# Rounds of a mixture-of-experts router: the inverse root of the variance moved from GpSimd to ScalarE and VectorE, the gate columns moved from VectorE to ScalarE

## The reference

```python
# layer 4 (x: 32 x 256 tokens of 128)
mu = mean(x); var = mean((x - mu)**2)
xn = (x - mu) * rsqrt(var + 1e-5) * gamma + beta
logits = xn @ Wr + br                       # 8 experts
top_vals, top_idx = top_k(logits, 2)
w = softmax(top_vals)                       # two gates per token
y = sum over the two experts e of w_e * (gelu(xn @ W1[e] + b1[e]) @ W2[e] + b2[e])
x = x + y
```

## Time and profile before

| what | value |
|---|---|
| time, median of 3 runs | 862.75 us (860.98 to 864.96) |
| the profiled execution: its own time | 861.31 us |
| its span, first to last instruction | 859.5 us |
| busy: TensorE, VectorE, ScalarE, GpSimd | 688.8, 618.1, 431.6, 310.8 us |
| mean granted TensorE clock | 0.697 |

### The profile page before, as it was taken

One profiled execution on the slowest core, in us unless ns is written; L12 is line 12 of the kernel. 1 busy time (PEld: TensorE's weight loads), 2 busy tenths in 40 slices (PEclk: granted clock), 3 DMA queues, 4 the chain that ended last, 5 costly groups with the idle time before them and its releaser, 6 DMA issues.

```text
span 859.5 us, 23527 instructions
## 1 busy us (share of the span) xinstructions
PE 688.8 (80%) x7545; PEld 494.4 (58%) x7545; DVE 618.1 (72%) x3004; ACT 431.6 (50%) x1572; POOL 310.8 (36%) x486
## 2 busy tenths in 40 slices
PE   0895898888887878788888888987783699998993
PEld 0774665545444445454545454576672388887883
DVE  5334777777777777777777777476775299998994
ACT  1113555444444444545454545244442288887882
POOL 4700112222232322232212112228776355555553
PEclk9997655555555555555555555689987699999997
DMA  4993111111111011111110111445522333443430
GB/s 128 163 233 120 32 32 45 32 44 32 42 31 43 31 40 34 40 33 41 32 43 31 43 31 31 135 122 171 159 93 81 112 93 105 109 114 96 112 87 1
DMA packets 75404, 64.39 MB, mean 75 GB/s; under 512 B 8344, under 2 KB 72189, under 8 KB 75309
## 3 DMA queue, kind: packets, MB, share of 16 engines
q1 hardware_dynamic: 67715, 50.31, 22.4%
q0 software_dynamic: 5984, 12.74, 4.2%
q10 hardware_dynamic: 1636, 0.48, 0.3%
HBM read 37.94 MB, written 27.32 MB: 76 GB/s over the span
## 4 chain that ended last, share of the span: by engine, by line
PE 42%; DVE 28%; ACT 17%; issue 9%; POOL 1%; another core or an unknown queue 1%; DMA 0%; DVEq 0%; SPq 0%; POOLq 0%; ACTq 0%
PE pb L813 10%; DVE pb L1462 8%; ACT tanh_c L1132 5%; DVE h L1464 5%; ACT GC L1128 4%; PE pb L1014 4%; ACT S L1130 3%; PE pb L850 3%; PE pb L1016 2%; PE pb L1015 2%; PE pb L1030 2%; PE pb L1031 2%; PE pb L1029 2%; ACT adjT L1147 2%; PE pb L727 2%
## 5 line engine op out<-in xcount | busy, mean ns | idle before, releaser
L813 PEld LDWEIGHTS pb<-h,vp 128*128 128x128 bf16 x3840 | 142.5, 106 | 190.7 <-DVE h L1464 187.7
L813 PE MATMUL pb<-h,vp 128*128 128x32 f16 x3840 | 171.5, 190 | 54.7 <-DVE h L1464 41.8
L691 POOL DMA_INDIRECT out<-outb,out_i x91 | 92.5, 1016 | 83.4 <-DVE outb L1647 62.1
L782 PE MATMUL pb<-xbuf,us 128*128 128x256 f32 x198 | 117.5, 699 | 0.0
L1128 ACT ACTIVATE GC<-pb 128x32 f32<-128x32 f32 x256 | 51.0, 199 | 130.1 <-PE pb L813 130.1
L1462 DVE TENSOR_TENSOR_SCAN pb<-S,GC 128x64 f32<-128x64 f32 x256 | 77.3, 302 | 32.5 <-ACT S L1130 18.5
L1132 ACT ACTIVATE tanh_c<-pb 128x32 f32<-128x32 f32 x256 | 50.5, 197 | 96.0 <-DVE pb L1462 96.0
L1464 DVE SCALAR_TENSOR_TENSOR h<-S,tanh_c 128x32 f16<-128x32 f32 x256 | 49.2, 192 | 67.4 <-ACT tanh_c L1132 67.4
L1635 DVE SCALAR_TENSOR_TENSOR glo<-Gl,pw,ghi 128x512 f16<-128x512 f32 x91 | 68.4, 752 | 19.0 <-ACT ghi L1244 11.6
L1014 PE MATMUL pb<-xT,w 128*128 128x128 f16 x364 | 66.4, 221 | 10.5 <-issue 5.5
L679 POOL DMA_INDIRECT xs_d<-stg,slot x64 | 62.9, 983 | 31.3 <-issue 17.7
(11 more groups left out here) (331 smaller groups left out, 1629.0 us busy)
## 6 DMA issues: line engine op xcount, KB each, us to landing
Xp<-xs_d SPq DMA_DIRECT2D x91, 130.0 KB
adjn<-in_adj SPq DMA_DIRECT2D x32, 256.0 KB, 2.7
x_d<-x2s SPq DMA_DIRECT2D x33, 128.0 KB, 1.8
y_d<-ys SPq DMA_DIRECT2D x33, 128.0 KB, 1.8
X<-in_x SPq DMA_DIRECT2D x4, 912.0 KB, 18.4
xs_d<-zrow SPq DMA_DIRECT2D x1, 3640.0 KB, 13.8
yr<-y_d SPq DMA_DIRECT2D x8, 256.0 KB
x2r<-x_d SPq DMA_DIRECT2D x8, 256.0 KB
```

Of the source, the lines that this page charges most:

```text
L691: pool.indirect_dma_start(out_rows, bass.IndirectOffsetOnAxis(out_i[t % 4][:, 0:1], 0), outb[t % 4][:], None, bounds_check=B * T - 1, oob_ ...
L782: mm(o, us[:, q, :], xbuf[:], start=False, stop=False, skip_group_check=True)
L813: return mm(o, vp[p][:, q, :], h[:], start=False, stop=True, skip_group_check=True)
```

## The change

In rounds 2 to 7 the inverse root comes by another way. VectorE stores a quarter of the variance term (rounds 0 and 1 keep the whole one and GpSimd's power). ScalarE's `take_root` takes the square root of it; the two one-element activations around it put ScalarE's table loads where they stand. VectorE's `scale(F)` then makes one correction step: with v the stored quarter and r the root, `v/r + r` is the corrected whole root, and its reciprocal is `rs_m`. `nb_m` follows at once, so it is made at the end of rows(F) and no longer inside route. GpSimd keeps only the powers of rounds 0 and 1. The gate columns `0.5 +- 0.5*tanh` are written by ScalarE behind the tanh, and GpSimd's send waits for them (`gates_set`).

```diff
@@ GpSimd @@
                 if half == 0:
                     pool.wait_ge(slot_ready, F + 1)
+                    pool.wait_ge(gates_set, F + 1)
...
             for F in range(NF):
                 send(F, 0)
-                if F + 2 < NF:
-                    norm_scale(F + 2)
                 send(F, 1)
@@ ScalarE @@
             def router_tanh(F):
                 act.wait_ge(dif_ready, F + 1)
                 av(th[F % 2][:], hdif[F % 2][:], ACT.Tanh).then_inc(th_ready, 1)
+                act.wait_ge(th_ready, F + 1)
+                av(stg[F % NBUF][:, :, 2 * P], th[F % 2][:], ACT.Identity, scale=half_k, bias=half_k)
+                av(stg[F % NBUF][:, :, 2 * P + 1], th[F % 2][:], ACT.Identity, scale=minus_k[:, 0:1], bias=half_k).then_inc(gates_set, 1)
+
+            def take_root(F):
+
+                av(spare[:, 0, F:F + 1], ident[:, 0:1], ACT.Sqrt)
+                act.wait_ge(m_aggr, F + 1)
+                av(root[F % 2][:], ve_m[F % 2][:], ACT.Sqrt).then_inc(root_ready, 1)
+                av(spare[:, 1, F:F + 1], ident[:, 0:1], ACT.Tanh)
...
                     normed_evacuate(2 * F + 2)
                     normed_evacuate(2 * F + 3)
+                    if F + 2 < NF:
+                        take_root(F + 2)
@@ VectorE @@
-                v.tensor_scalar(ve_m[F % 2][:], mv_m[F % 2][:, :, 1], LN_EPS, SC ** -2, ALU.add, ALU.mult).then_inc(m_aggr, 1)
+                v.tensor_scalar(ve_m[F % 2][:], mv_m[F % 2][:, :, 1], LN_EPS, SC ** -2 * (0.25 if F >= 2 else 1.0), ALU.add, ALU.mult).then_inc(m_aggr, 1)
...
+            def scale(F):
+
+                k = F % 2
+                dve.wait_ge(root_ready, F - 1)
+                link(v.reciprocal(quot[:], root[k][:]))
+                link(v.tensor_tensor(quot[:], ve_m[k][:], quot[:], ALU.mult))
+                link(v.tensor_tensor(quot[:], quot[:], root[k][:], ALU.add))
+                link(v.reciprocal(rs_m[k][:], quot[:]))
                 v.scalar_tensor_tensor(out=nb_m[k][:], in0=mv_m[k][:, :, 0], scalar=-1.0, in1=rs_m[k][:], op0=ALU.mult, op1=ALU.mult).then_inc(nb_ready, 1)
...
-                if F + 1 < NF:
-                    shift(F + 1)
+                if F == 0:
+                    shift(1)
...
-                dve.wait_ge(th_ready, F + 1)
-                v.tensor_scalar(stg[n][:, :, 2 * P], th[k][:], half_k, half_k, ALU.mult, ALU.add)
-                v.tensor_scalar(stg[n][:, :, 2 * P + 1], th[k][:], minus_k[:, 0:1], half_k, ALU.mult, ALU.add)
...
                 if F + 2 < NF:
                     rows(F + 2)
+                    scale(F + 2)
```

More of the change, by code:

```diff
@@ L253, in build @@
         mv_m, ve_m, rs_m, nb_m = (ring(n, 2, [P, NT] + s) for n, s in (("mv_m", [2]), ("ve_m", []), ("rs_m", []), ("nb_m", [])))
-        half8 = sb("half8", [P, NT])
+        half8, quot, root = sb("half8", [P, NT]), sb("quot", [P, NT]), ring("root", 2, [P, NT])
+        spare = sb("spare", [P, 2, NF])
         lg, top, top_i = sb("lg", [P, NT, E]), sb("top", [P, NT, E]), sb("top_i", [P, NT, E], U32)
@@ L305, in build @@
         adj_loaded = [sem(f"adj_loaded{i}") for i in range(2)]
-        (ht_ps, hts_ready, c_ps, x3_ready, m_aggr, rs_ready, nb_ready, xh_ready, xhT_ps, xnT_ready,
-         logits_ps, brg_ps, brg_ready, dif_ready, th_ready, oneh_ready, rank_ps, rank_read, count_ps, slot_ready, wrg_ready,
+        (ht_ps, hts_ready, c_ps, x3_ready, m_aggr, rs_ready, root_ready, nb_ready, xh_ready, xhT_ps, xnT_ready,
+         logits_ps, brg_ps, brg_ready, dif_ready, th_ready, gates_set, oneh_ready, rank_ps, rank_read, count_ps, slot_ready, wrg_ready,
          beta_ready, fold_ps, folded_w, biased, prep_ready, squares_ready, folded_ready, mx_ps, mx_ready, powers_ready, tri_ready,
@@ L311, in build @@
          xt_ps, xT_ready, xl_ready, l1_ps, gelu_ready, ghi_ready, glo_ready, l2_ps, out_ready) = (sem(n) for n in (
-            "ht_ps", "hts_ready", "c_ps", "x3_ready", "m_aggr", "rs_ready", "nb_ready", "xh_ready", "xhT_ps", "xnT_ready",
-            "logits_ps", "brg_ps", "brg_ready", "dif_ready", "th_ready", "oneh_ready", "rank_ps", "rank_read",
+            "ht_ps", "hts_ready", "c_ps", "x3_ready", "m_aggr", "rs_ready", "root_ready", "nb_ready", "xh_ready", "xhT_ps", "xnT_ready",
+            "logits_ps", "brg_ps", "brg_ready", "dif_ready", "th_ready", "gates_set", "oneh_ready", "rank_ps", "rank_read",
             "count_ps", "slot_ready", "wrg_ready", "beta_ready", "fold_ps", "folded_w", "biased", "prep_ready", "squares_ready", "folded_ready",
@@ L1533, in shift @@
                 dve.wait_ge(rs_ready, F + 1)
+                v.scalar_tensor_tensor(out=nb_m[k][:], in0=mv_m[k][:, :, 0], scalar=-1.0, in1=rs_m[k][:], op0=ALU.mult, op1=ALU.mult).then_inc(nb_ready, 1)
+            def scale(F):
[5 more added lines that the diff above has]
+                link(v.reciprocal(rs_m[k][:], quot[:]))
                 v.scalar_tensor_tensor(out=nb_m[k][:], in0=mv_m[k][:, :, 0], scalar=-1.0, in1=rs_m[k][:], op0=ALU.mult, op1=ALU.mult).then_inc(nb_ready, 1)
```

## The result

The changed kernel takes 880.05 us (median of 4 runs, 879.73 to 883.87) against 863.36 us of the kernel before, measured beside it: ratio 1.021, 95% interval 1.018 to 1.024. That is slower by 17 us, outside the predicted range of 857 to 871. Its profiled execution took 880.01 us, with a span of 878.2.

A forecast was written before the change was run, and what follows sets the result against it. The rounds were taken as bound by a VectorE-ScalarE-TensorE loop setting the last slots, not by busy GpSimd. lg delays of +4.05, less 0.6 and 0.25, gave +3.2 us: 864.5 or 866.0 by baseline, forecast 865.5, range 857 to 871.

The forecast's parts named there:

- The terms of the chain: Per round, from last evacuation to lg: 0.2 for gates, 1.66 to the root, 0.96 on VectorE, together +2.82 us.
- Root after the evacuation: On ScalarE in each round with a root: it is ready 1.66 us after the evacuation ends.
- The table load: On ScalarE behind the last evacuation: 1.28 us, next activation 0.02 behind it; the load back is hidden.
- The semaphore: Last term of the root's path on ScalarE: 0.05 us.
- The figure of the Trainium skill: ScalarE's table switch at about 2.66 us: root some 1.4 us later each round, sum near +9; not adopted.
- Gate writes: Two ScalarE activations ahead of normalise's second half: 0.28 us each, 0.6 with the wait; evacuations 0.2 later, between 0 and 0.8.
- the sum of +3.2 us: Net delay over the rounds: lg delays of +4.05, less 0.6 for nb_m and 0.25 for VectorE's gate writes.
- the removed part: Six powers leave GpSimd's queue, 9.5 us, worth nothing while VectorE's last slots come as late as now.
- inside the stall: Rounds 1 and 3: VectorE's existing stalls ahead of lg cover the root's longer path, so each adds 0.
- signs of being wrong: Wrong if "remote" waits vanish or move, the first reciprocal doesn't wait, or the rounds' granted clock is well under 0.9.
- The rival on the stalls: VectorE's stalls in the rounds belong to GpSimd's power and go with it: -1.7 to -5.3 us, 857.4; chance 0.25.
- The clock rival: TensorE waits longer in the rounds and its clock falls: 1.7 us per such round, about +6, 871; chance 0.20.

The follow-up runs named there:

- e1: The kernel before with ScalarE writing the gate columns, powers left on GpSimd: 864.44 us, ratio 1.003.
- e4: The kernel before with ScalarE's root and table loads added behind the evacuations, result unused, powers left on GpSimd: 861.74 us, ratio 1.000.
- e9: The changed kernel as it is, measured again in a group without late signals: 844.5 us, ratio 0.999 to the kernel before.
- e15: The changed kernel with an idle GpSimd power between the halves of each round's transfers, rounds 0 to 5; late signals: 866.52 us, ratio 1.006.
- e17: The changed kernel with scale moved from ahead of route (the suspected place) into route, transfers in runs of eight; late signals: 887.19 us, ratio 1.024.
- warm: The changed kernel with three idle matmuls ahead of each round's places: ratio 0.995 to 0.996 without late signals, 1.018 with them.
- e18: The changed kernel with three idle matmuls ahead of each round's places, in a group with late signals: 876.6 us, ratio 1.018.
- e11: The changed kernel with an idle GpSimd power between the halves of each round's transfers, without late signals: 846.72 us, ratio 1.001.
- in_route: The changed kernel with scale moved inside route, where shift was, transfers in runs of eight: ratio 0.995 to 0.996 without late signals, 1.024 with them.
- e7: The changed kernel with scale inside route and an idle GpSimd power between each round's transfer halves, without late signals: 845.45 us, ratio 1.001.
- e6: The changed kernel with scale inside route, transfers in runs of eight, without late signals: 840.2 us, ratio 0.995.

## Why the prediction was wrong, point by point

**The terms of the chain were right.** Root after the evacuation: 595.61 - 593.99 = 1.62 us, predicted 1.66. scale: 596.75 - 595.64 = 1.1 with nb_m's own 0.23, and 0.9 to nb_m's start; predicted 0.96 in all. The table load: 1.28 us, 0.02 behind the evacuation's end, and the next activation 0.02 behind the load. The semaphore, for which the sum had 0.05 us, took 595.64 - 595.61 = 0.03. The figure of the Trainium skill ("ScalarE: Activation LUTs", section "What ACT_TABLE_LOAD costs"), 2.66 us for a switch, is not what this trace shows: from the evacuation's end to the root's start are 595.42 - 593.99 = 1.43 us, with a small activation in it. Gate writes: 0.40 us each, started 0.3 apart, predicted 0.28 and inside the bounds. e1 prices them all at 1.003 (1.000 to 1.006), e4 the loads at 1.000. No run has the sum of +3.2 us by itself, but e9 has the whole longer chain at 844.5, so this sum is not where 17 us were missed.

**The step that failed is the one on the removed part:** "Six powers leave GpSimd: 9.5 us of its queue. By the above this is worth nothing as long as the last slots come as late as now". I put it at nothing, since I counted the power as GpSimd time and asked who waits for GpSimd; and I took the slots' lateness as given, which it wasn't. The power did something else: it stood between the fourth and the fifth transfer of a round. Without it GpSimd issues all eight at the pitch of 1.27 us. In the groups with late signals these signals are late from 3.4 us of such a run on, and the last engines are released 2.4 to 2.7 us after its last transfer. The chain of a round has its hts and lg just there, and as the next run starts only with the next slots, rounds 2 to 6 all fall into the pattern: lg is late in five rounds running (598.59 to 664.63), where it was in two before. So the last slots, which were to come some 3 us later, came 18.2 later. e15 shows it by giving the pause back, e17 by moving the rival's suspect and losing as much as ever, e9 by a group in which the signals are on time. Whether it is the pause that helps or something else in the power isn't shown, since no other pause was tried.

**The rounds "inside the stall".** I took the stalls of rounds 1 and 3 as fixed places on the clock, in which the root would hide for nothing. They are tied to the transfers, and move with them. The prediction had named "remote" waits that lie elsewhere and a granted clock well under 0.9 as signs of being wrong, and both were there: lg is held in five rounds and not in two, and the mean clock of 590 to 665 is 0.82.

**The rival on the stalls had the place right and the sign wrong.** "The stalls of VectorE belong to the power", since they ended as a power did. They ended 2.58 and 2.26 us after the last transfer of a run, and the power filled that time; in the changed kernel the delay is the same, 2.43 to 2.63, with no power there. I read the coincidence as guilt; that ScalarE stalled while transfers ran (592.05), and that the powers behind runs of four had no stall beside them, spoke for the other reading, and both could be seen in the trace before. The case that would follow, faster by 5 us, came out backwards where the stalls are.

**The clock rival came true as a symptom.** TensorE idles for 4 us and more ahead of the places (30.1 in 7, the longest 5.8) and its clock falls to 0.78 and 0.89 where it was 0.77 and 1.00. Its price of 1.7 us for a round would make 8 or more of the 17 us; warm lifts the clock above that of the kernel before and gives back about 3 (e18). In the changed kernel the fallen clock goes with the late signals: where these are missing (e9) TensorE's waits ahead of the places are 11.1 us in 6, the longest 2.3, and the clock is 1.00 from 560 to 620 (0.89 from 620 to 635). That is no rule for every kernel: in e1, with one late signal, the clock costs 2 us in one group of matmuls.

**What the whole is made of.** The same program took 880.05 us in the first measurement and 844.5 in e9, 35.5 apart; the kernel before 863.36 and 845.23, 18.1 apart. The first gap is the wider by 17.4, which is the loss of 16.7 and the 0.7 gained in e9. Not all of either gap is late signals in the rounds. From the start of the last transfer to the end the nine traces with late signals take 186.0 to 190.2 us (before 187.7, the changed kernel 188.2), the eleven others 179.0 to 180.7 (e9: 841.89 - 662.18 = 179.7). So some 8 us part the two kinds of group in the pages, with and without powers, and drop out of the ratios; why the pages differ wasn't followed. Of the 38.1 us between the profiled executions of the changed kernel, 29.6 lie ahead of the last transfer. In a group without late signals the power costs the changed kernel 2.2 us (e11 against e9), and costs in_route 5.3 (e7 against e6); where signals are late it saves 13 (1.021 less 1.006, times 863; two groups). No version here beats the kernel before in both kinds of group: in_route gains 0.5% in one and loses 2.4% in the other.

**Still open** is the mechanism: why signals are late in four groups of eight, and whether it is the number of transfers in flight, their descriptors or their landings that does it. Nor do late signals explain the whole of what parts the two kinds of group: e1 has one and is no faster, by its clock. One thing goes with them. In e9 the profile has a landing for the row transfers, in the changed kernel's first profile it has none (view of DMA issues, 565 to 690, which leaves out the changed kernel's last two; number of issues, then median us to landing, first e9 and then the changed kernel):

```profile
xs_d<-stg,slot POOLq DMA_INDIRECT x64, 2.5
```

```profile
xs_d<-stg,slot POOLq DMA_INDIRECT x62
```

The same holds for every other trace: all eleven without late signals have the landing, none of the nine with late signals has it. So the records are themselves incomplete where signals are late, while the 2.5 us to landing is about the delay by which the last release follows the last transfer. The Trainium skill ("NOTIFIC — the notification-queue block", section "Overflow: three behaviours, one of which stalls the engine") says that a full queue of such records can stall the engine that makes them. That would fit one cause for both, and no run here shows it. Nor does any run settle whether the loss is there without such records: every run of these groups lists a granted clock, so none seems to be without them. It wasn't tried whether a cheaper pause than a power, or one between rounds as well, would do better.

## What to carry to other kernels

Before an instruction is taken out of a queue as "hidden", ask what it keeps apart, not only how long it takes: on GpSimd six powers of 1.67 us, each between four and four indirect transfers, were worth 13 us of the whole in some groups of runs. Waits with no releaser that the profile knows are not noise to be held fixed: set each beside what the other queues did in the 10 us before it, and a rule shows, or doesn't, in the trace that you already have. And measure a change more than once, at other times and on other chips: here its ratio is 1.021 in one group and 0.999 in another, and each interval is narrow.

## What the runs showed of the hardware that was not expected

- One program has two levels: the kernel before takes 862.0, 862.9, 865.3 and 862.2 us in the groups with late signals and 844.6, 845.2, 845.7 and 846.5 in those without, nothing between. Chip number 0 is in both lists (862.0 and 845.7).
- In a late stretch VectorE, ScalarE and SyncE went on within 0.01 us of each other (602.88, 602.89), even where the work waited for was VectorE's own. GpSimd's transfers kept their pitch of 1.27 us.
- A load of ScalarE's tables took 1.28 us, with 0.02 us ahead of it and 0.02 behind it (594.01 to 595.31), and six rounds of two loads left the time as it was (e4: 1.000, 0.998 to 1.002).
- A reciprocal of 128x8 on VectorE took 0.20 us, against 1.14 for the 160 elements of the earlier trace rows; the sum had 0.23 with its link.
